# A decoder layer on one core: the sums over keys split by a part of the value projection, and the first tile's projections moved ahead of the other loads

## What is computed

```python
q, k, v = x @ Wq.T + bq, x @ Wk.T + bk, x @ Wv.T + bv      # 16 heads of 32; rope on q, k
att = softmax(q k / sqrt(32))        # per token, over heads
x = layernorm(x + (att v) @ Wo.T + bo)
# the second block attends over time, with gates: C = (q k / sqrt(32)) * D,
# D = exp(log decay - running maximum), lower triangle only
h = (C / (max(|C.sum(-1)|, exp(-max)) + eps)) @ ctx
x = layernorm(x + headwise_norm(h) * ln_scale)
# the third: of 8 experts the one with the highest gate; rank-8 update
x = layernorm((1 - g) * x + g * (bias_e + degen_e (update_e (x - debias_e))))
```

## Time and profile before

| | us |
|---|---|
| median of 3 runs | 2005.21 |
| lowest, highest | 2002.34, 2016.72 |
| the profiled execution, its own time | 2007.69 |
| its span, first to last instruction | 2006.2 |

### The profile page before, as it was taken

One profiled execution on the slowest core, in us unless ns is written; L12 is line 12 of the kernel. 1 busy time (PEld: TensorE's weight loads), 2 busy tenths in 40 slices (PEclk: granted clock), 3 DMA queues, 4 the chain that ended last, 5 costly groups with the idle time before them and its releaser, 6 DMA issues.

```text
span 2006.2 us, 67466 instructions
## 1 busy us (share of the span) xinstructions
PE 1854.5 (92%) x27656; PEld 1536.5 (77%) x27656; DVE 1551.2 (77%) x3898; ACT 778.7 (39%) x2193; POOL 774.0 (39%) x779
## 2 busy tenths in 40 slices
PE   0889999999999999999999999999999999999985
PEld 0678888887887887788788878878878877887863
DVE  4456777888878788887888888777887788887776
ACT  1223344344434434443443444344344344344341
POOL 1124344344334334433433443343344344344342
PEclk9988898999989999999999999899998999999895
DMA  4111122212221221211222122212212212221110
GB/s 137 59 65 55 65 65 76 75 65 77 79 74 58 78 74 63 79 71 64 75 79 74 63 79 77 75 58 78 74 63 74 74 63 74 74 83 58 63 54 27
DMA packets 53829, 141.14 MB, mean 70 GB/s; under 512 B 8767, under 2 KB 10431, under 8 KB 45578
## 3 DMA queue, kind: packets, MB, share of 16 engines
q1 hardware_dynamic: 53770, 140.31, 20.4%
HBM read 122.98 MB, written 17.30 MB: 70 GB/s over the span
## 4 chain that ended last, share of the span: by engine, by line
PE 83%; DVE 6%; ACT 6%; issue 3%; SPq 1%; POOL 0%; DMA 0%; POOLq 0%; ACTq 0%; DVEq 0%
PE bank L477 13%; PE bank L355 13%; PE bank L356 13%; PE bank L358 12%; PE bank L347 8%; PE quad L467 4%; PE bank L434 3%; PE bank L446 3%; PE bank L491 3%; PE bank L503 3%; PE bank L448 3%; PE bank L351 2%; ACT x_high L563 2%; DVE x L931 1%; ACT gs L599 1%
## 5 line engine op out<-in xcount | busy, mean ns | idle before, releaser
L713 POOL TENSOR_TENSOR ex<-ex,w_rec 128x512 f32<-128x512 f32 x64 | 67.6, 1056 | 766.5 <-DVE w_rec L827 766.5
L621 ACT ACTIVATE Dx<-Mb,a_col 128x128 f32<-128x128 f32 x1024 | 312.8, 395 | 0.0
L725 POOL TENSOR_TENSOR h_rs<-h_ve,half_neg 128x16 f32<-128x16 f32 x64 | 201.3, 3146 | 220.9 <-DVE h_ve L913 220.9
L477 PE MATMUL bank<-c,Dx 128*128 128x33 f32 x2048 | 270.3, 295 | 16.5 <-ACT LT L651 14.5
L477 PEld LDWEIGHTS bank<-c,Dx 128*128 128x128 f32 x2048 | 262.9, 211 | 23.8 <-ACT LT L651 21.5
L594 ACT ACTIVATE x1T<-bank 128x512 f32<-128x512 f32 x64 | 38.3, 598 | 356.1 <-PE bank L347 356.1
L892 DVE SCALAR_TENSOR_TENSOR Dx<-quad,Dx 128x512 f32<-128x512 f32 x256 | 159.0, 683 | 11.4 <-PE quad L467 2.8
L739 POOL TENSOR_TENSOR rs<-ve,half_neg 128x1 f32<-128x1 f32 x192 | 106.0, 552 | 153.3 <-DVE ve L848 153.2
L718 POOL TENSOR_SCALAR_AFFINE_SELECT Dx<-Dx 128x512 f32<-128x512 f32 x256 | 160.1, 638 | 5.5 <-ACT Dx L621 5.5
L355 PE MATMUL bank<-wv_high,x_high 128*128 128x512 f32 x256 | 151.0, 590 | 0.0
L347 PE MATMUL bank<-id_sb,x 128*128 128x128 f32 x512 | 85.3, 290 | 54.9 <-DVE x2sq L933 53.0
(11 more groups left out here) (157 smaller groups left out, 4551.4 us busy)
## 6 DMA issues: line engine op xcount, KB each, us to landing
Mb<-m_rows SPq DMA_DIRECT2D x64, 1024.0 KB, 4.6
xb<-in_x SPq DMA_DIRECT2D x256, 64.0 KB
xr<-in_x SPq DMA_DIRECT2D x64, 256.0 KB, 2.6
cb<-in_ctx SPq DMA_DIRECT2D x64, 256.0 KB, 3.6
out_dram<-yo SPq DMA_DIRECT2D x64, 256.0 KB, 2.4
Dx<-in_wq SPq DMA_DIRECT2D x4, 256.0 KB, 4.7
Dx<-in_wk SPq DMA_DIRECT2D x4, 256.0 KB, 5.5
Mb<-in_wv SPq DMA_DIRECT2D x4, 256.0 KB, 6.2
```

Of the source, the lines that this page charges most:

```text
L477: last = mm(bank[6 + h // 8][:, (h % 8) * HD:(h % 8 + 1) * HD], Dx[t.parity()][:, h % 4, h // 4, :], c1[:, h, :], start=True, stop=True)
L621: last = go(Dx[t.parity()][:, j, n, :], Mb[t.parity()][:, h, :], ACT.Exp, bias=a_col[t.parity()][:, h:h + 1], scale=-1.0)
L725: tt(h_rs[:], h_ve[:], half_neg[:], ALU.pow).then_inc(s.hrs_sb, 1)
```

## The change

Two parts. In the steps: TensorE's 16 sums over keys are no longer issued in one piece. The first five go ahead, then the bias and the first four matmuls of the value projection, then the other eleven sums, then the remaining eight matmuls of the projection. The waits of `m_H` and of `p_v` stay ahead of their first matmuls. `H_ps` is still raised by the sixteenth sum, `v_ps` by the last matmul of the projection.

In front: x of tile 0, the identity and the biases are loaded first, then the weights, each of the four matrices with a semaphore of its own; context, the other constants and the residual follow. Tile 0 is transposed as soon as x and the identity are there. VectorE works bias by bias and matrix by matrix; the low part of x comes after the first. `p_q`, `p_k`, `p_v` and `a_proj` of the peeled steps each wait only for their own weights and bias. The experts' constants are multiplied out after step 0, and summed by TensorE at the head of step 2 (`shift`).

```diff
-PADS = 7
+PADS = 6
...
+        first = [(id_sb[:], ident), *[(bias_in[n], bqkv[:, n * E:(n + 1) * E]) for n in range(3)]]
...
             load_x(Tile(0))
-            load_res(Tile(0))
-            load_ctx(Tile(0))
+            for dst, src in first:
+                sp.dma_start(dst, src).then_inc(s.first_in, 16)
             for n, w in enumerate((wq, wk, wv, wo)):
                 for c in range(CH):
-                    sp.dma_start(w_in[n][c], w[c * P:(c + 1) * P]).then_inc(s.w_in, 16)
+                    sp.dma_start(staged[n][c], w[c * P:(c + 1) * P]).then_inc(s.w_in[n], 16)
+            load_ctx(Tile(0))
+            for dst, src in consts:
+                sp.dma_start(dst, src).then_inc(s.const_in, 16)
+            load_res(Tile(0))
             load_x(Tile(1))
...
             def p_q(t):
-                if t.k == 0 and t.regs is None:
-                    pe.wait_ge(s.low_set, 4)
+                if t.regs is None:
+                    pe.wait_ge(s.low_set, 1)
+                    pe.wait_ge(s.bias_step, 5)
+                    pe.wait_ge(s.ones_set, 1)
...
             def p_v(t):
+                if t.regs is None:
+                    pe.wait_ge(s.low_set, 3)
+                    pe.wait_ge(s.bias_step, 15)
+                    if t.k > 0:
+                        pe.wait_ge(s.shift_set, 1)
                 edge(pe, t, (s.xhigh_sb, 0), (s.xlow_sb, 0), (s.VG_sb, 1), (s.QT_sb, 0), (s.fn1_sb, 4))
                 bias(4, 2)
-                product(4, x_high, x_low, 2, False).then_inc(s.v_ps, 1)
+                high_part(4, x_high, 2, 0, 2)
+
+            def p_v_rest(t):
+                high_part(4, x_high, 2, 2, CH)
+                low_part(4, x_low, 2).then_inc(s.v_ps, 1)
...
-                for h in range(H):
+
+            def heads(t, lo, hi):
+                for h in range(lo, hi):
                     last = mm(bank[6 + h // 8][:, (h % 8) * HD:(h % 8 + 1) * HD], Dx[t.parity()][:, h % 4, h // 4, :],
                               c1[:, h, :], start=True, stop=True)
-                last.then_inc(s.H_ps, 1)
+                return last
...
-            pe.wait_ge(s.const_in, CONST_IN)
-            pe.wait_ge(s.prod_set, 3)
-            pe.wait_ge(s.pads_set, PADS)
-            for c in range(CH):
-                last = mm(bank[4][:, 0:NW], ones_f[:], wx_prod[:, c, :], start=(c == 0), stop=(c == CH - 1))
-            last.then_inc(s.shift_ps, 1)
-            pe.wait_ge(s.shift_set, 1)
-            pe.wait_ge(s.bias_step, 15)
-            pe.wait_ge(s.center_set, 11)
+            pe.wait_ge(s.first_in, FIRST_IN)
+
+            def shift():
+
+                pe.wait_ge(s.prod_set, 3)
+                pe.wait_ge(s.QT_sb, 2)
+                pe.wait_ge(s.VG_sb, 1)
+                for c in range(CH):
+                    last = mm(bank[4][:, 0:NW], ones_f[:], wx_prod[:, c, :], start=(c == 0), stop=(c == CH - 1))
+                last.then_inc(s.shift_ps, 1)
 
             def step(a):
                 b, c, d, e, f, g = [a.older(n) for n in range(1, 7)]
+                if a.regs is None and a.k == 1:
+                    pe.wait_ge(s.const_in, CONST_IN)
+                    pe.wait_ge(s.pads_set, PADS)
+                    pe.wait_ge(s.center_set, 11)
+                if a.regs is None and a.k == 2:
+                    shift()
                 if c.real():
                     m_gate(c)
                 if b.real():
                     a_S(b)
                 if d.real():
                     m_H(d)
+                    heads(d, 0, 5)
                 if b.real():
                     p_v(b)
+                if d.real():
+                    heads(d, 5, H).then_inc(s.H_ps, 1)
+                if b.real():
+                    p_v_rest(b)
                     m_cT(b)
...
-            act.wait_ge(s.const_in, CONST_IN)
-            act.wait_ge(s.w_in, 16 * 4 * CH)
-            act.wait_ge(s.scale_set, 1)
+            act.wait_ge(s.scale_set, 2)
             for n in range(4):
+                act.wait_ge(s.w_in[n], 16 * CH)
                 for c in range(CH):
-                    last = go(w_high[n][:, c, :], w_in[n][c], ACT.Copy)
+                    last = go(w_high[n][:, c, :], staged[n][c], ACT.Copy)
                 last.then_inc(s.high_set, 1)
-            act.wait_ge(s.low_set, 4)
-            act.wait_ge(s.pads_set, PADS)
+                if n == 0:
+                    p_xT(Tile(0))
...
+            split_bias(0)
+            split_weight(0)
+            p_low(Tile(0))
+            split_bias(1)
+            split_weight(1)
+            split_bias(2)
+            split_weight(2)
```

More of the change, by code:

```diff
@@ L235, in bass_decoder @@
             ve3_sb rs3_sb yo_sb""".split()
-        four = "Dx_sb Dm_sb C_sb".split()
+        four = "Dx_sb Dm_sb C_sb w_in".split()
         two = "x_in c_in r_in mb_in".split()
@@ L241, in bass_decoder @@
         s = namedtuple("Semaphores", semaphores)(**semaphores)
-        w_in = [[Dx[0][:, i].rearrange("p c n -> p (c n)") for i in range(CH)],
+        staged = [[Dx[0][:, i].rearrange("p c n -> p (c n)") for i in range(CH)],
                 [Dx[1][:, i].rearrange("p c n -> p (c n)") for i in range(CH)],
@@ L248, in bass_decoder @@
         bias_rest = [t[0:1, :] for t in (x1[0], x1[1], x2[0])]
+        first = [(id_sb[:], ident), *[(bias_in[n], bqkv[:, n * E:(n + 1) * E]) for n in range(3)]]
+        FIRST_IN = 16 * len(first)
         consts = [
-            *[(bias_in[n], bqkv[:, n * E:(n + 1) * E]) for n in range(3)], (bo_sb[:], bo.broadcast_to([P, E])), (id_sb[:], ident),
+            (bo_sb[:], bo.broadcast_to([P, E])),
             (wg_sb[:], w_gate.rearrange("(m c p) n -> p m c n", p=P, c=CH)), (bg_sb[:], b_gate),
@@ L351, in bias, with high_part, low_part @@
                 mm(bank[b][:], ones_bf[:], bias3[:, n * E:(n + 1) * E], start=True, stop=False)
+            def high_part(b, high, n, lo, hi):
+                for c in range(lo, hi):
+                    mm(bank[b][:], high[:, c, :], w_high[n][:, c, :], start=False, stop=False)
+                    mm(bank[b][:], high[:, c, :], w_low[n][:, c, :], start=False, stop=False)
+            def low_part(b, low, n):
+                for c in range(CH):
+                    last = mm(bank[b][:], low[:, c, :], w_high[n][:, c, :], start=False, stop=c == CH - 1)
+                return last
             def product(b, high, low, n, first):
@@ L419, in a_proj @@
             def a_proj(t):
+                if t.regs is None:
+                    pe.wait_ge(s.low_o_set, 1)
                 pe.wait_ge(s.Olow_sb, upto(t))
@@ L675, in step @@
                     p_VG(b)
-                if a.real():
+                if a.real() and not (a.regs is None and a.k == 0):
                     p_xT(a)
@@ L1046, in _, with split_weight @@
-            last.then_inc(s.prod_set, 1)
-            tt(wx_prod[:, :, 2 * nw:NW], wx_sb[:, :, 2 * nw:NW], wx_sb[:, :, 2 * nw:NW],
-               ALU.mult).then_inc(s.prod_set, 2)
-            dve.wait_ge(s.shift_ps, 1)
-            nc.vector.tensor_copy(wx_shift[:], bank[4][:, 0:NW]).then_inc(s.shift_set, 1)
-            dve.wait_ge(s.shift_set, 1)
-            for n in range(3):
-                dve.wait_ge(s.high_set, n + 1)
-                for c in range(CH):
-                    last = tt(w_low[n][:, c, :], w_in[n][c], w_high[n][:, c, :], ALU.subtract)
-                last.then_inc(s.low_set, 1)
+            def split_weight(n):
+                dve.wait_ge(s.high_set, n + 1)
+                dve.wait_ge(s.w_in[n], 16 * CH)
+                for c in range(CH):
+                    last = tt(w_low[n][:, c, :], staged[n][c], w_high[n][:, c, :], ALU.subtract)
+                last.then_inc(s.low_set, 1)
@@ L1059, in step, with keep_shift @@
+            def keep_shift():
+                dve.wait_ge(s.shift_ps, 1)
+                nc.vector.tensor_copy(wx_shift[:], bank[4][:, 0:NW]).then_inc(s.shift_set, 1)
             def step(a):
                 b, c, d, e, f, g = [a.older(n) for n in range(1, 7)]
+                if a.regs is None and a.k == 2:
+                    keep_shift()
+                if a.regs is None and a.k == 4:
+                    dve.wait_ge(s.shift_set, 1)
                 if b.real():
@@ L1110, in step @@
                     m_scan(b)
+                if a.regs is None and a.k == 0:
+                    products()
             steps(dve, step)
```

55 lines of the change are left out of this document (35 added, 20 removed).

## The result

The changed kernel takes 2073.88 us, the median of 3 runs (2073.42 to 2081.55), against 2005.21 before: 1.034 times as long (95% interval 1.027 to 1.041). I had predicted 1889 (1872 to 1915) and had given "slower" 2 chances in 100.

A forecast was written before the change was run, and what follows sets the result against it. TensorE, busy 92% of the span and partly at a low clock, was taken to bound the kernel. 2007.7 - 88 - 28 = 1891.7 us, given as 1889 because the profiled execution lay 2.5 us above the median; range 1872 to 1915.

The forecast's parts named there:

- Part one, 88 us: Steps: splitting the sums keeps TensorE's clock up in nearly all steps, saving 88 us (bounds nothing to 92).
- 3 or 4 were allowed for: First steps that hold sums (3 to 6): other waits there may still lose 3 or 4 us to low clock.
- What the split costs, 0 us: Steps: `H_ps` comes 1.15 us later, but VectorE's idle time before `y` swallows the delay: 0 us.
- VT late: Rival, steps: copy Hs over 0.8 us later makes TensorE wait before transposes; 33 us more, 2038 us; chance 0.02.
- Part two, 28 us: Front: reordered loads and VectorE work start tile 0's scores near 32 us, 31 us earlier; net gain 28 us.
- lower bound of 22: Front: gain of 22 us if all pieces beside GpSimd are slowed and Wq lands at 13.
- the low part of Wv: Front, VectorE: 2.50 us, plus a share of 2 us added for pieces slowed beside GpSimd.
- The third rival: Front bound by loading, Wq's pieces spread among later loads: 10 us gained in place of 28, 1907 us; chance 0.05.
- The one wait inserted, on `shift_set`: Written-out steps: named as the only wait inserted, for those steps only; no time was given for it.
- The forecast's own tests: Right if: Wv matmuls 450 ns, step clock 0.99 or 1.00, steps 28.2 us, tile 0 scores at 30 to 34 us.

The follow-up runs named there:

- split_only: Kernel before with only the sums split 5 and 11, no instruction added, old front: 1924.80 us, 0.956.
- fit: Changed kernel with TensorE's new waits kept only in the first steps that need them, 50 instructions fewer ahead of the loop: 1916.53 us, 0.955 of the kernel before.
- fit_trim: fit without the waits on `pads_set` in the written-out steps, 9 instructions fewer ahead of the loop: 1900.18 us, 0.946 of the kernel before.
- front_only: fit with all 16 sums in one piece again, so the new front alone: 1988.67 us, 0.989 of the kernel before.
- before_pad55: Kernel before with 110 long-fulfilled waits (55 instructions) added ahead of TensorE's first matmul: 2194.14 us, 1.090.
- after_pad190: Changed kernel with 380 fulfilled waits (190 instructions) added ahead of TensorE's first matmul: 1910.00 us, 0.953 of the kernel before.
- before_pad25: Kernel before with 50 fulfilled waits (25 instructions) added ahead of TensorE's first matmul: 2074.43 us, median of two runs.
- split_11_5: after_pad190 with 11 sums ahead of the first part of the value projection and 5 behind it: 2110.35 us, 1.051 of the kernel before.
- split_8_8: after_pad190 with 8 sums ahead of the first part of the value projection and 8 behind it: 1939.30 us, 0.966 of the kernel before.

## Why the prediction was wrong

- **Part one, 88 us: right.** split_only gained 87.7 us. In its loop, as in those of fit and fit_trim, the clock is 1.00. That it agrees to 0.3 us is luck: the interval is 79 to 97. In the first steps split_only still has two low phases of 10.24 us (from 138.70 and 200.14), which lose some 10 us where 3 or 4 were allowed for. A mean clock of 0.979 over 1925.3 us means 81 us at the low level in split_only's profile, one of 0.936 over 2006.2 means 257 us before; half of the difference is 88 us.
- **What the split costs, 0 us: right.** In a step without low clock the copy Hs, `h_n` and the transposes of the value stand in the changed kernel as follows, and TensorE takes VT at 1021.82 without a wait:

```profile
1018.32 0.67 ACT L672 ACTIVATE Hs<-bank 128x264 f32<-128x264 f32 x2 [1.71 <-PE bank L508]
...
1019.02 0.18 DVE L946 SCALAR_TENSOR_TENSOR h_n<-Hs,eFM 128x16 f32<-128x16 f32 x1 [1.09 <-ACT Hs L672]
...
1020.27 0.72 DVE L835 STREAM_TRANSPOSE VT<-bank 128x512 f32<-128x512 f32 x1 [0.42 <-PE bank L363]
...
1021.82 0.60 PE L350 MATMUL bank<-id_sb,VT 128*128 128x128 f32 x4
...
1023.32 0.75 DVE L1037 SCALAR_TENSOR_TENSOR y<-x,g_rest,bank 128x512 f32<-128x512 f32 x1 [0.96 <-PE bank L534]
```

  VT waits for its own projection (L363) and not for the sums, and VectorE still idles 0.96 us ahead of `y`, as in the earlier trace rows. The rival "VT late" is ruled out.
- **Part two, 28 us: right in size, perhaps some us too high.** The profiles of fit and split_only differ by 1925.3 - 1898.6 = 26.7 us. By the ratios of fit_trim and split_only, 0.946 and 0.956, it is some 21 us, just under the lower bound of 22; by front_only 24. The scores start at 33.88, forecast 30 to 34. One term was too small: the low part of Wv took 6.09 us beside GpSimd's 6.60, not 2.50 and a share of 2. The four lie beside it nearly all the time, 1.58 us each in the mean. The Trainium skill, SBUF — State Buffer, section "Who interferes with whom", has a VectorE instruction with two inputs in SBUF contend with a GpSimd instruction that reads SBUF; the 1.58 us against 0.69 for the same instruction alone (wk_low, 686 ns) agree with it. The third rival, a front bound by loading, falls: Wq was there at 11.13.
- **The step that failed.** "The one wait inserted, on `shift_set`, is for the written-out steps only", and no term for the other waits of `p_q`, `p_k`, `p_v` and `a_proj` there. I costed 55 instructions ahead of the loop at nothing and gave no reason for it. None of my rivals was about where the loop lies. They cost 182 us in the kernel before (before_pad55), and 1910.00 - 13 for after_pad190 without its padding, some 1897 us, set against 2073.88 gives 177 us here (184 if one allows for the kernel before, which took 2012.01 us beside after_pad190 and 2005.21 beside the changed kernel).
- **How the 169 us of the loop add up.** Fit has the same 52 steps in 1465.5 us, the changed kernel in 1634.9. In these, TensorE's stalls with releaser "issue" are 58.9 at L475, 36.8 at L441, 15.0 at L508 and 5.3 at L428, 116 us. The low phases of this stretch sum to 140 us in the trace, half of which is lost, 70 us. Part of it is saved again, as other waits have shrunk: in these steps that of the transposes of `x2` for VectorE (L350, by `x2sq`) is 27.0 us in the changed kernel and 44.8 in fit. That leaves 168 of the 169. It is an estimate: the terms are not independent of each other.
- **Sum.** The 177 is itself taken from the 2073.88, so it tests nothing. With the 182 of before_pad55, measured without the split and the new front, 2005.21 - 88 - 28 + 182 = 2071, and 2073.88 was measured. That this is so near is partly luck: half of the 182 is low clock in a kernel whose sums are unsplit, and the two kernels need not pay the same.

The forecast's own tests would have misled: scores at 34 us and Wv's matmuls at 484 ns were right, and the clock of 0.96 over the steps looked as though the sums were still at fault. Only the list of waits and the row of queue 8 told the stalls apart.

## What to carry to other kernels

Before moving anything in a kernel with a hardware loop, read the row of instruction packets and count the pieces of 256 instructions that the loop touches, from its start to its end (seen here for TensorE's loop alone): the start counts as well as the length. An instruction ahead of such a loop is not free even when its wait is long fulfilled. If a loop is within some tens of instructions of the next piece, keep what stands ahead of it fixed, by trimming or by padding, and look for stalls with releaser "issue" right behind the branch.

## What was not expected

- A loop of 1758 TensorE instructions that lies in seven pieces of 16 KB is loaded once. Lying in eight, from place 68, it is loaded anew in each turn, with nine packets, and the kernel takes some 9% longer (182 us of 2012, 177 of 1897). Between the two it depends: from place 18, with 16 instructions to spare in the seventh piece, 5 turns of 26 were loaded again in one execution, from 38 it was 13 in one. In the changed kernel the stalls stand at four places of the turn, 0.6 us in the mean at L508 and 2.3 at L475.
- Where the loop is loaded in some turns only, the stall at the head of such a turn is longer: 3.4 us in the mean in before_pad25 and 3.7 in front_only, in place of 2.3.
- The low clock can last 10 us with TensorE busy without a break, where further sums follow shortly on the fall (split_11_5, split_8_8). In the kernel before, with all sums ahead of the projection, it lasted 3.4 us in 24 of 33 falls and 6.8 in the others.
- A low clock comes in two ways here. In the kernel before TensorE was busy for 3.44 of 3.44 us before the fall; in the changed one it fell after 2.11 us of idle time. It is so throughout the 52 steps: in the 3.4 us ahead of a fall TensorE was idle for 0.2 us at most in all 33 of the kernel before, for 0.9 to 2.5 us in all 27 of the changed one.
